# Rotated queries and key moved from a TensorE transpose to a fifth plane of the block placement, two units ahead

## What is computed

```python
q, k, v = x @ Wq.T, x @ Wk.T, x @ Wv.T            # per head of 128
q = rope(rmsnorm(q, q_norm_w), pos); k = rope(rmsnorm(k, k_norm_w), pos)
k_all, v_all = concat(cache_k, k), concat(cache_v, v)      # 512 + 128 keys
scores = einsum('bqhd,bkhd->bhqk', q, k_all) / sqrt(128)   # masked where not valid
o = einsum('bhqk,bkhd->bqhd', softmax(scores), v_all)
x = x + o.reshape(...) @ Wo.T
```

## Time and profile before

| | |
|---|---|
| median of 3 runs | 1165.55 us (1165.37 to 1169.18) |
| the profiled execution | 1164.61 us, span 1162.9 us |
| busy share of the span | PE 97%, PEld 84%, DVE 73%, ACT 59%, POOL 41% |
| granted TensorE clock, mean | 0.990 |
| DMA | 277.30 MB in 125672 packets, mean 238 GB/s |
| share of 16 DMA engines | SP's queue 47.7%, ACT's 16.1%, POOL's 11.4% |

### The profile page before, as it was taken

How to read it: one execution, slowest core, us unless ns; L and a number is a source line. 1 busy time by engine, 2 the same in 40 slices (tenths; PEclk the granted TensorE clock), 3 DMA queues, 4 the chain that set the end, 5 groups by cost and what they waited for, 6 DMA issues and landing times. The chain is left out here.

```text
span 1162.9 us, 27332 instructions
## 1 busy us (share of the span) xinstructions
PE 1124.7 (97%) x6112; PEld 974.8 (84%) x6112; DVE 844.8 (73%) x2167; ACT 683.1 (59%) x1914; POOL 475.6 (41%) x570
## 2 busy tenths in 40 slices
PE   5999799999999999999999999999999999999996
PEld 3555688898988898988898988898988898988884
DVE  2334677877887877887877887877887877777772
ACT  2223466666666666666666666666666666666661
POOL 6852244443444443444443444443444443333320
PEclk9999799999999999999999999999999999999999
DMA  6673488787887787787787787787787788777774
GB/s 181 190 270 140 151 244 250 236 258 251 256 265 247 239 262 247 253 264 248 238 261 247 255 264 246 238 259 254 251 266 243 238 256 258 229 245 234 239 223 142
DMA packets 125672, 277.30 MB, mean 238 GB/s; under 512 B 13656, under 2 KB 79320, under 8 KB 124634
## 3 DMA queue, kind: packets, MB, share of 16 engines
q1 hardware_dynamic: 78536, 194.28, 47.7%
q10 hardware_dynamic: 35970, 46.15, 16.1%
q0 software_dynamic: 11152, 36.72, 11.4%
HBM read 186.92 MB, written 90.18 MB: 238 GB/s over the span
## 5 line engine op out<-in xcount | busy, mean ns | idle before, releaser
L697 ACT ACTIVATE prob<-prob,low 128x640 f32<-128x640 f32 x256 | 210.1, 826 | 133.0 <-DVE low L1151 133.0
L931 PE MATMUL ps_o<-prob_t,v_raw 128*128 128x256 f32 x1024 | 243.6, 381 | 6.5 <-DMA v_raw<-v_rows_dram,v_row 6.5
L1151 DVE CUSTOM_DVE_ANT_0 prob<-ps_s,mask,q_gain 128x640 f32<-128x640 f32 x256 | 215.6, 879 | 36.7 <-PE ps_s L772 36.7
L931 PEld LDWEIGHTS ps_o<-prob_t,v_raw 128*128 128x128 f32 x1024 | 190.4, 191 | 30.8 <-DMA v_raw<-v_rows_dram,v_row 7.3
L1169 DVE STREAM_TRANSPOSE blocks<-prob 128x640 f32<-128x640 f32 x256 | 207.1, 828 | 2.0 <-ACT prob L702 2.0
L702 ACT ACTIVATE prob<-prob,inv 128x640 f32<-128x640 f32 x256 | 196.7, 816 | 0.6 <-DVE inv L1157 0.6
L770 PE MATMUL ps_s<-kt_hi,qt_hi 128*128 (+1 forms) x512 | 172.1, 336 | 5.3 <-DVE kt_lo L1072 3.8
L870 PE MATMUL ps_q<-w_hi,x_s 128*128 (+1 forms) x512 | 173.0, 398 | 0.0
L772 PE MATMUL ps_s<-kt_hi,qt_lo 128*128 (+1 forms) x512 | 160.5, 314 | 0.0
L771 PE MATMUL ps_s<-kt_lo,qt_hi 128*128 (+1 forms) x512 | 160.3, 313 | 0.0
L650 ACT ACTIVATE ot_hi<-ps_o 128x256 fp32r<-128x256 f32 x128 | 49.1, 384 | 175.7 <-PE ps_o L931 175.7
(11 more groups left out here) (134 smaller groups left out, 2156.6 us busy)
## 6 DMA issues: line engine op xcount, KB each, us to landing
blocks_placed<-blocks SPq DMA_DIRECT2D x128, 640.0 KB, 3.6
prob_t<-blocks_placed ACTq DMA_DIRECT2D x128, 320.0 KB, 5.2
prob_t<-blocks_placed SPq DMA_DIRECT2D x128, 320.0 KB, 6.4
x_s<-xt_split SPq DMA_DIRECT2D x64, 512.0 KB, 3.7
w_raw<-w_qkvo_dram SPq DMA_DIRECT2D x55, 320.0 KB, 3.8
w<-w_t_dram SPq DMA_DIRECT2D x8, 1024.0 KB, 5.2
xt_split<-x3t ACTq DMA_DIRECT2D x8, 512.0 KB, 3.9
w_raw<-w_qkvo_dram POOLq DMA_DIRECT2D x9, 320.0 KB, 4.1
```

The source lines that it names most:

```text
L697: nc.scalar.activation(prob[:, h, :], prob[:, h, :], ACT.Exp, bias=low[:, h:h + 1], scale=-1.0, accum_out=total[:, h:h + 1]).then_inc(exp_ ...
L931: mm = nc.tensor.matmul(ps_o[pair][:, 0:PAIR], v, turned_probs(c, pair), start=c == 0, stop=c == CH - 1)
L1151: nc.vector.tensor_tensor_reduce(out=prob[:, h, :], in0=ps_s[:, score_slot(h):score_slot(h) + KEYS], in1=mask[:, :], scale=q_gain[:, h:h + ...
```

## The change

The rotated queries and the rotated key (five tiles of 128x128, just the width of one head's 640 probabilities) no longer go through TensorE. DVE turns them in 32x32 blocks like a head's probabilities, into a fifth plane of `blocks` (plane 2, in the first of the two sends, which now carries three planes; the second carries two). They are placed by the same four transfers, and ACT and DVE read the high and low parts from `prob_t` in place of `ps_q` and `ps_kv`. The layout has one run of 32x5 numbers (640 bytes) per plane where it had one of 32x5x2 (1280 bytes) per pair of heads. Since the placed plane of unit n+1 comes with the probabilities of unit n-1, projection, rotation, norms and sums are now done for unit n+2 in step n. Both issuers also wait on `qt_lo_out` before they place, and DVE writes the low parts in front of the fourth head's block turn. Units 0 and 1 keep the TensorE transposes (`not pv` is step 0), and unit 2 is projected and rotated at the end of step 0. One more weight chunk is loaded ahead, and `v_next` has four slots.

```diff
-AHEAD = B + 1
+AHEAD = B + 2
+PLANES = GROUP + 1
+ROT_PLANE = 2
...
-        blocks_dram = nc.dram_tensor("blocks_placed", [2 * NB, BLOCK, NB, CH * 2 * BLOCK], F32).ap()
+        blocks_dram = nc.dram_tensor("blocks_placed", [PLANES * NB, BLOCK, NB, CH * BLOCK], F32).ap()
...
-def place_blocks(n, first=False):
+def place_blocks(n, ahead=True, first=False):
 
     sp.wait_ge(blocks_turned, GROUP * n + 2)
     sp.nop(nofuse=True)
+    if ahead:
+        sp.wait_ge(rot_blocked, n + 1)
+        sp.nop(nofuse=True)
...
-    send_blocks(sp, 0)
+    send_blocks(sp, 0, ROT_PLANE + 1)
     sp.wait_ge(blocks_turned, GROUP * (n + 1))
     sp.nop(nofuse=True)
-    send_blocks(sp, 1)
+    send_blocks(sp, ROT_PLANE + 1, PLANES)
     sp.wait_ge(blocks_out, 32 * (n + 1))
     sp.nop(nofuse=True)
     if not first:
         sp.wait_ge(pv_done, 2 * n)
+        sp.nop(nofuse=True)
+        sp.wait_ge(qt_lo_out, n + 2 if ahead else UNITS)
         sp.nop(nofuse=True)
...
+def rotated_high(u):
+    act.wait_ge(pt_in, 16 * NB * (u - 1))
+    act.wait_ge(scores, GROUP * u)
+    copy(as_blocks(qt_hi[:, :]), placed_queries)
+    copy(as_key_blocks(keys_of(kt_hi, u, CACHE, KEYS)), placed_key).then_inc(qt_hi_out, 1)
...
-def place_rest(n, first=False):
+def place_rest(n, ahead=True, first=False):
     act.wait_ge(blocks_out, 32 * (n + 1))
     if not first:
         act.wait_ge(pv_done, 2 * n)
+        act.wait_ge(qt_lo_out, n + 2 if ahead else UNITS)
...
     score_pair(n, 0)
+    if not pv:
+        project_queries(n + 1, turned=True)
+    elif ahead:
+        project_queries(n + 2)
+    score_pair(n, 1)
+    if not pv:
+        project_new_key(n + 1)
+    elif ahead:
+        project_new_key(n + 2)
     if not last:
-        project_queries(n + 1)
-    score_pair(n, 1)
-    if not last:
-        project_new_key(n + 1)
         turn_cached(n + 1)
     if out:
         put_out(n - 2)
-    if not last:
+    if not pv:
         turn_rotated(n + 1)
+        project_queries(n + 2, turned=True)
+        project_new_key(n + 2)
     if pv:
         values(n - 1, first=not out)
...
+def turn_rotated(u):
+
+    dve.wait_ge(q_summed, u + 1)
+    dve.wait_ge(key_scaled, u + 1)
+    nc.vector.transpose(blocks[:, ROT_PLANE, :, :, :].rearrange("p j c q -> p c j q"),
+                        rot[:, :, :].rearrange("p c (j k) -> p c j k", j=NB)).then_inc(rot_blocked, 1)
```

More of the change, by code:

```diff
@@ L484, in _ @@
                     load_chunk(0, 1)
[L485 removed]
+                    with pool.Fori(0, AHEAD // 2 - 1) as j:
                         for at in (0, 1):
@@ L532, in move_new_value, with step @@
                         nc.gpsimd.tensor_copy(v_new[:, :], next_value(u)).then_inc(vn_moved, 1)
-                    def step(n, weights, keys, last, first=False, second=False):
+                    def step(n, weights, keys, ahead, first=False, second=False):
                         if not first:
@@ L707, in place_rest, with query_norms, step @@
                             act.wait_ge(pv_done, 2 * n)
+                            act.wait_ge(qt_lo_out, n + 2 if ahead else UNITS)
                         for j in range(NB // 2, NB):
                             place_rows(act, j)
-                    def step(n, last, head=True, out=True, first=False):
+                    def query_norms(u, first=False):
+                        query_squares(u, range(GROUP))
+                        key_squares(u)
+                        new_value(u, first=first)
+                    def step(n, last, head=True, out=True, first=False, second=False, ahead=True):
                         if head:
@@ L719, in step @@
                         normalize(n, 1)
-                        if not last:
-                            query_squares(n + 1, range(GROUP))
-                            key_squares(n + 1)
-                            new_value(n + 1, first=not out)
+                        if not out:
+                            query_norms(n + 1, first=True)
+                        elif ahead:
+                            query_norms(n + 2, first=not head)
                         exps(n, 2)
                         exps(n, 3)
-                        if not last:
+                        if not out:
                             scale_key(n + 1)
+                        elif ahead:
+                            scale_key(n + 2)
                         normalize(n, 2)
@@ L731, in step @@
                             cached_high(n + 1, first=not out)
-                            rotated_high(n + 1)
+                            if out:
+                                rotated_high(n + 1)
+                            else:
+                                first_rotated_high(n + 1)
+                        if not out:
+                            query_norms(n + 2, first=True)
+                            scale_key(n + 2)
                         if out:
@@ L941, in put_out, with step @@
                         mm.then_inc(out_proj, 1)
-                    def step(n, last, out=True, pv=True):
+                    def step(n, last, out=True, pv=True, ahead=True):
                         pe.wait_ge(qt_lo_out, n + 1)
@@ L1176, in step @@
                         dve.wait_ge(gain_done, n + 1)
-                        if not first:
+                        if out:
                             dve.wait_ge(blocks_turned, GROUP * n)
@@ L1196, in step @@
                         inverse(n, 3)
+                        if out and ahead:
+                            turn_rotated(u)
                         if head:
@@ L1228, in _ @@
                     set_mask(0)
-                    step(0, True, False, head=False, out=False, first=True)
+                    step(0, True, False, head=False, out=False)
                     step(1, True, False, head=False)
```

163 lines of the change are left out of this document (102 added, 61 removed).

## The result

The changed kernel takes 1271.83 us (median of 5 runs, 1266.08 to 1276.95), the kernel before 1165.37 in the same session (1164.43 to 1169.18): a ratio of **1.0927**, 95% interval 1.0898 to 1.0956. It is slower, 30 us above the forecast of 1242 us and inside the range of 1190 to 1305. The profiled execution took 1266.08 us (span 1264.3), 101.4 us of span more than before (1162.9).

The account below looks back on a forecast made before the run. TensorE paced the old kernel at 15.86 us a unit; after the change a loop through ACT, DVE and the sends would bind at 17.1. 1164.6 + 75 (60 units) + 3 (net, mainly start and end) = 1242 us, range 1190 to 1305.

Parts of the forecast that it names:

- the loop: First exponential (E), DVE and ACT work to fourth turn, second send, `place_rest`, next exponential: 14.8 us before, 17.1 after.
- in a loop that TensorE no longer paces this cover is gone: On DVE, the new block turn of 0.78 us is no longer covered by the 0.91 us idle ahead of the add.
- by more than a tenth or two: On ACT, the high parts at about E+9.05 would delay the low parts by at most a tenth or two.
- to `place_rest` 4.04, as the second send again carries two heads: From the fourth turn's end to `place_rest`: 4.04 us as before, up to 0.7 faster or 0.3 slower.
- rival 1: The second send lands 0.7 us sooner with nothing in front: unit 16.4 us, total time 1200 us; chance 0.18.
- The placement: Four transfers with 2560 runs of 640 bytes land after 9.0 us, where 7.3 before, hidden with 1.5 us left.
- The start, +4.2: Unit 2's projection between the scores of units 0 and 1 adds 2.8 us for queries, 1.4 for key and value.
- The end, -1.3: At the end, unit 62's step loses the rotation, 1.3 us, from the loop.
- Rival 3: TensorE's clock falls to half after pauses of 1.8 us a unit: unit 18.1 us, total time 1302 us; chance 0.07.
- Rival 2: The placement becomes the loop from a landing of 10.5 us on: unit 19.0 us, total time 1360 us; chance 0.10.
- Rival 4: TensorE still bounds, the next exponentials not feeling the later send: unit 15.32 us, total time 1134 us; chance 0.10.

Follow-up runs that it names:

- b_low_front: The kernel before with only its three low parts moved in front of the fourth head's block turn: 1188.14 us, ratio 1.0199.
- low_behind: The changed kernel with the three low parts moved back behind the fourth head's block turn: 1272.8 us, ratio 1.0940.
- three_sends: The changed kernel with heads 0 and 1 sent once turned, the rotated plane by itself, heads 2 and 3 last: 1231.56 us, ratio 1.0583.
- b_turn_and_front: The kernel before with low parts in front of the fourth turn and a block turn of `rot` into a tile nothing reads: 1183.74 us, ratio 1.0152.
- three_low_behind: low_behind with the blocks sent in three transfers, the rotated plane by itself behind its own turn: 1220.55 us, ratio 1.0473.
- two_buffers: three_low_behind with two DRAM buffers for the blocks, so the first send needn't wait for the placement before to land: 1238.75 us, ratio 1.0639.
- light_loads: three_low_behind with the loads of x and weights cut to 64 columns, so values differ: 1208.41 us, ratio 1.0390.
- sp_places: The changed kernel with all four placing transfers issued by SP, none by ACT: 1372.04 us, ratio 1.1798.

## Why the prediction was right, and where it wasn't

**What bounds, and the loop.** Right in kind, and lucky in the number. A loop through ACT, DVE, the sends and ACT again holds every unit, TensorE idles ahead of the value products, and b_low_front shows the forecast loop by itself. The steps that I added up are there: exponential to end of fourth turn 12.1 forecast, 12.17 measured; turn to placing 4.04 against 4.02 in the mean; placing to exponential 0.97 against 1.03. Round 17.1 against 17.24: 56 rounds of 0.14 are 8 us of the miss. But they aren't what the round waits for. With the low parts taken out from in front of the fourth turn it stayed at 17.22 (low_behind), so the 1.37 us that the sum charged for them cost the changed kernel nothing. What it waits for is the first send, held for the rotated plane: that turn ends at 613.41, E+8.7, the first send leaves 0.2 us later, the placing follows after 7.4, the exponential after 1.0, together 17.3. My own path, freed of that, is the 16.63 of three_sends. The two paths lie 0.6 us apart, and that is why a sum over the wrong one came out close.

**The step "in a loop that TensorE no longer paces this cover is gone".** Wrong. I put the fifth turn's whole 0.8 us on the loop. b_turn_and_front shows that it costs nothing beside the low parts in front: the two idle times on DVE shrink by what it takes. In the changed kernel the difference to b_low_front is 12.17 against 12.07, 0.1 us. The sum came out because the high parts on ACT, which I thought would not hold the low parts up "by more than a tenth or two", let them start at E+9.8 at the earliest, and DVE with the turn arrives at E+9.9. Two chains end together there, and adding up one of them hides the other. On the second path the turn does count: the first send can't leave before it ends.

**The step "to `place_rest` 4.04, as the second send again carries two heads".** The number held by luck, its reason didn't. I argued from the second send alone. It is 4.02 since the first send, held until the rotated plane is turned, is still under way: with that send earlier (three_sends) the same second send is placed after 3.32. So rival 1, with its 3.3 us and 16.4 a unit, is what the change would have been with the first send split and heads 0 and 1 not waiting for the rotated plane. Its sum said 1200 and three_sends took 1231.6: the mean round of 16.63 makes 13 us of that, start and end some 11, and the median lies 7 above the profiled run.

**The placement.** Forecast 9.0 us to landing, and 9.3 to 9.4 seen; off the loop, as forecast. But I looked only at who reads it. The next unit's first send also waits for this landing, and that is the third path, 16.5 us, above TensorE's 15.32 by itself. With 1.6 MB out and 1.6 MB back in each unit, no order that was tried got below it by much: low_behind, three_low_behind, two_buffers and light_loads each took away one holder of the round, and it went from 17.24 to 16.2 at the least.

**The start, +4.2.** Too small: +9.2 to unit 0's placing, and +7.8 by unit 4, of which four rounds of 1.38 are 5.5. I counted TensorE's work alone and not who is queued behind it. DVE's timeline there, then SP's queue, and the first matmul and the clock of unit 2's projection:
```profile
131.48 1.57 DVE L1238 STREAM_TRANSPOSE blocks<-prob 128x640 f32<-128x640 f32 x2 [0.90 <-ACT prob L738]
...
139.59 0.69 DVE L1156 TENSOR_TENSOR rot_a<-ps_q,cos_q 128x512 f32<-128x512 f32 x1 [5.10 <-PE ps_q L921]
...
144.69 0.85 DVE L1245 STREAM_TRANSPOSE blocks<-rot 128x640 f32<-128x640 f32 x1 [1.11 <-ACT rot L701]
```
```profile
145.63 1.20 SPq L286 DMA_DIRECT2D blocks_placed<-blocks  x2
```
```profile
134.56 0.77 PE L921 MATMUL ps_q<-w_hi,x_s 128*128 128x512 f32 x1 [2.96 <-DVE kt_lo L1135]
```
```profile
136.00:138.00 2.00, 2.00 (x6) 1.62 (x5) 0.00 (x0) 0.00 (x0) 0.00 (x0) 0.50 0.00 0
```
Unit 0's four heads are turned at 133.05, 5.9 us before they were in the kernel before (137.40 + 1.57); no run here shows why. But `place_blocks(0)` waits for the rotated plane of unit 2, whose projection begins only at 134.56, at half clock (0.50, the 1.2 GHz level, behind a pause of 2.96 us). From 133.05 it is 12.5 us until that turn ends, and the sends of unit 0 wait for it on SP.

**The end, -1.3.** Wrong sign: +6.8 from unit 60's placing. The view of PE shows the waits of the last two units, 62 and 63, for their placements, and SP's queue what lies between:
```profile
1231.72 3.35 PE L986 MATMUL ps_o<-prob_t,v_raw 128*128 128x256 f32 x8 [3.09 <-DMA prob_t<-blocks_placed]
...
1249.42 3.75 PE L986 MATMUL ps_o<-prob_t,v_raw 128*128 128x256 f32 x8 [7.76 <-DMA prob_t<-blocks_placed]
```
```profile
1231.55 0.92 SPq L286 DMA_DIRECT2D blocks_placed<-blocks  x2
1239.25 0.87 SPq L291 DMA_DIRECT2D prob_t<-blocks_placed  x2
```
The last unit's placing at 1239.06 (ACT) and 1239.25 (SP) stands 7.9 us behind its fourth turn, where it was 4.1 before. The turn ended at 1231.15, but both sends go out only at 1231.55, as unit 62's placement lands (1231.47), and land at 1239.04. That is the third path at the end of the kernel: two placements and the sends between them stand one behind the other, with no unit's work to cover them, which the sum left out. Of the miss of the profiled run, 1266 - 1242 = 24 us, the rounds, the start and the end make some 8 each; the median lies another 5.8 us above that run.

**Rival 3, the clock.** It happens in part: behind the wait of 2.77 us at 630.78 the granted clock was 0.57 over 4 us, and eight value matmuls took 3.46 us in place of 1.99. Over the steady stretch it is still 0.99, and over the whole run 0.973 (0.990 before); sp_places, with the longest rounds, had 0.94. The loop doesn't go through TensorE, so little of it need reach the round; what it costs was not tried. The Trainium skill (TensorE: Matmul & The Clock Gate, HAM oscillation — how this bites in real kernels) describes a kernel that waits for DMA in each round and whose clock swings to the low level each time. This trace doesn't agree: TensorE waits 1.9 us on average in nearly each unit, and the steady clock stays at 0.99.

**Rivals 2 and 4.** Rival 2 did not happen: the placement landed after 9.25 us in the mean, below its point of 10.5. In sp_places the landing is above that point and the time near its sum (1360 against 1372), but there the third path gives the same round, so it isn't shown to be rival 2's chain. Rival 4 is excluded by b_low_front: the later send is felt.

## What to carry to other kernels

When an edit lengthens a loop across engines, list every chain that ends at the loop's last step, with its own end time, and see which is how far behind: here DVE's order, the wait of the first send and the landing of the placement ended within about 1 us of each other, and taking out one gave nothing (low_behind) or 0.6 us of a round (three_sends). A sum that comes out right doesn't show that its path is the one that bounds: take one of its terms away and see if the time moves. A transfer has two kinds of followers: those who read what it brings, and those who overwrite what it reads. And a new wait in a loop must be read once at the first and once at the last turn of the loop, where what it waits for is not ahead of time.

## What the runs showed of the hardware

- The same four placings of 640-byte runs landed 12.0 us (mean) after the first issue when all came from SP's queue, 9.25 when SP and ACT issued two each. The last issue is 1.5 us behind the first in the one case and 0.5 in the other, so issuing explains about 1 us of the 2.7.
- Fewer, longer packets in the placement did not help the run: with 512 of 3200 bytes in place of 2560 of 640 it was 1.1% longer, and with two DRAM buffers 35 us longer. In the second pair the DMA share fell, from 0.93 to 0.87 over 400 to 1000 us, and the time rose all the same: a lower share was not a faster kernel. Both edits also cut the sends into shorter runs.
- The last send of 640 KB was followed by the placing 3.13 us after its last turn where the send before it had left 4.5 us earlier (b_low_front), after 4.0 where 960 KB had left 3.3 us earlier (the change), and after 5.4 where they had left 1.9 us earlier (low_behind).
